# Second layer's front: context products of 129 columns per half, summed over the tiles in PSUM

## The chip, the core and the metric

The kernel runs on one core of a Trainium2 chip. Its time is the device time of one execution in microseconds (us); three runs of the kernel before gave a median of 2431.36 us (2429.86 to 2431.77).

## The reference, cut to what matters

Two layers of a graph network work on 2500 nodes of 256 features. Each layer has a graph part, a linear attention over all nodes, and a mixture of experts. The change is in the second layer's linear attention, whose sum over all nodes is `context`:

```python
q = jnp.einsum('bnc,oc->bno', x, Wq).reshape(B, N, h, d).transpose(0, 2, 1, 3)
kv = jnp.einsum('bnc,oc->bno', x, Wkv).reshape(B, N, 2, h, d)
k = kv[:, :, 0].transpose(0, 2, 1, 3)
v = kv[:, :, 1].transpose(0, 2, 1, 3)
q = jax.nn.elu(q) + 1.0
k = jax.nn.elu(k) + 1.0
k_sum = k.sum(axis=2)
D_inv = 1.0 / jnp.maximum(jnp.einsum('bhnd,bhd->bhn', q, k_sum), 1e-06)
context = jnp.einsum('bhnd,bhne->bhde', k, v)
attn = jnp.einsum('bhnd,bhde->bhne', q, context) * D_inv[..., None]
```

There are h = 8 heads of d = 32 features. Only k and v of the same head meet: of the 256 x 256 sum of k times v, the kernel needs the eight 32 x 32 blocks on the diagonal, and beside them the sum of k itself (`k_sum`).

## The kernel before

The program is a row of stages, each a function with a block of its own, and all engines meet at a barrier between two stages. The change is in `front1`, which runs from about 1260 to 1405 us. The nodes are cut into T = 20 tiles of 128. For each tile TensorE turns the normalised rows (`turn`, into `p_t`), multiplies them by the weights of k and v (`p_kv`, 512 columns, line 1799), of q (`p_q`, line 1805), of the graph part's scores (16 further columns of `p_q`, line 1809) and of the graph part's features (`p_h`, 512 columns, line 1818). All is fp32, and each fp32 product stands as two records in the trace, with two weight loads.

VectorE and ScalarE make the features of k and q: `take(t)` on VectorE writes `neg`, the negative part, and `v_m`, which is v with rows past the last node zeroed and a 257th column of ones (`live`); ScalarE takes the exponential of `neg` (line 1759); `features(t)` on VectorE writes `k_f` (line 1668) and `qT`. `context_product(t)` then multiplies each 128-feature half of `k_f` by all 257 columns of `v_m` (line 1789) into `p_c`, and VectorE adds the 2 x 257 columns of `p_c` to `context` in SBUF (line 1677, `add_context`).

The order on each engine is the order of the code. In round t TensorE issues `p_kv`, `p_q`, the scores, `turn(t + 1)`, `context_product(t - 1)` and `p_h`. VectorE issues `take(t)`, `norm(t + 2)`, `features(t)` and `add_context(t - 1)`. The waits that matter: `kv_used`, set by the `k_f` instruction, lets TensorE overwrite `p_kv` in the next round and lets the context product start; `c_ready` tells VectorE that `p_c` is full, and `c_used` tells TensorE that it has been added.

Ahead of the loop VectorE clears `context` (line 1685) and makes `w_a`, the weights of the scores, on which TensorE's first round waits (`wa_ready`). Behind it VectorE copies the diagonal blocks from `context` to `cb` (lines 1712 and 1713) and finds the range of the scores; ScalarE and SyncE store `z`, and the barrier ends the stage. TensorE's last product of the stage (`spread`, line 1824) goes to `p_c` too.

Of the kernel before, what the change touches and what calls it, by code (L numbers as in the profile page):

```python
# [8 lines left out]
ALU = mybir.AluOpType  # L9
# [4 lines left out]
P = 128  # L14
N = 2500
T = -(-N // P)
NP = T * P
LAST = N - (T - 1) * P
D = 256
# [8 lines left out]
H = 8  # L28
DH = D // H
# [1505 lines left out]
def front1(nc, io, st):  # L1535

    with ExitStack() as ctx:
        sb, ps, sem = tensors(nc, ctx)
# [12 lines left out]
        live = sb("live1", [P, T])  # L1551
        row = sb("row1", [P, 2, ROW1])
        neg = sb("neg1", [P, 2, 2 * D])
        k_f = sb("k_f1", [P, 2, D])
        v_m = sb("v_m1", [P, 2, D + 1])
        context = sb("context1", [P, 2, D + 1])
        ends = sb("ends1", [P, 2 * H])
        end = sb("end1", [2 * H, 1])
        diag = sb("diag1", [2 * H, 2 * H])
        ones = sb("ones1", [2 * H, P])  # L1560
# [7 lines left out]
        p_kv = ps("p_kv1", [P, 512])  # L1568
        p_q = ps("p_q1", [P, 512])
        p_c = ps("p_c1", [P, 2, 512])  # L1570
# [15 lines left out]
        neg_ready = sem("neg_ready1")  # L1586
        exp_ready = sem("exp_ready1")
        c_ready = sem("c_ready1")
        c_used = sem("c_used1")
        row_stored = [sem(f"row_stored{u}") for u in range(2)]  # L1590
        ends_ready = sem("ends_ready1")
        ends_turned = sem("ends_turned1")
# [1 line left out]
        spread = sem("spread1")  # L1594
# [36 lines left out]
        def _(dve):  # L1631
            link = Link(dve, dv)
# [17 lines left out]
            def take(t):  # L1650
                u = t % 2
                dve.wait_ge(kv_ready, t + 1)
                if t:
                    dve.wait_ge(exp_ready, t)
                dve.tensor_scalar(neg[:, u, 0:D], p_kv[:, 0:D], 0.0, None, ALU.min)
                link.inc(dve.tensor_scalar(v_m[:, u, 0:D], p_kv[:, D:], live[:, t:t + 1], None, ALU.mult))
                link.inc(dve.tensor_copy(v_m[:, u, D:D + 1], live[:, t:t + 1]))
                dve.wait_ge(q_ready, t + 1)
                dve.tensor_scalar(neg[:, u, D:], p_q[:, 0:D], 0.0, None, ALU.min).then_inc(neg_ready, 1)
                if t >= 2:  # L1660
                    dve.wait_ge(row_stored[u], 16 * (t // 2))
                dve.tensor_copy(row[:, u, HF:], p_q[:, D:D + H])
                dve.tensor_copy(st.s_all[:, t * 2 * H:(t + 1) * 2 * H], p_q[:, D:D + 2 * H]).then_inc(s_taken, 1)
# [6 lines left out]
                dve.scalar_tensor_tensor(out=st.qT[:, t * D:(t + 1) * D], in0=p_q[:, 0:D], scalar=0.0, in1=neg[:, u, D:],  # L1670
                                         op0=ALU.max, op1=ALU.add).then_inc(q_used, 1)

            def add_context(t):
                dve.wait_ge(c_ready, t + 1)
                if t:
                    dve.wait_ge(c_used, t)
                dve.tensor_tensor(context[:, :, :], context[:, :, :], p_c[:, :, 0:D + 1], ALU.add).then_inc(c_used, 1)

            norm(0)
            norm(1)  # L1680
            link(dve.tensor_tensor(diag_p[:, :], st.ident[:, :], st.iota[:, :], ALU.mult))
            link(dve.tensor_reduce(st.iota_p[:, :], diag_p[:, :], AX, ALU.add))
            link(dve.memset(live[:, :], 1.0))
            link(dve.tensor_copy(live[:, T - 1:T], st.rowmask[:, :]))
            link(dve.memset(context[:, :, :], 0.0))
            link(dve.memset(st.cb[:, :, :], 0.0))
            link(dve.memset(ones[:, :], 1.0))
            dve.wait_ge(w_in, 64)
# [8 lines left out]
            for t in range(T):  # L1697
                take(t)
                if t + 2 < T:
                    norm(t + 2)  # L1700
                features(t)
                if t:
                    add_context(t - 1)
            add_context(T - 1)
            dve.wait_ge(c_used, T)
            dve.wait_ge(s_taken, T)
            dve.wait_ge(dv, link.base + link.k)

            for g in range(4):
                r = slice(g * DH, (g + 1) * DH)  # L1710
                for c in range(2):
                    link.inc(dve.tensor_copy(st.cb[r, c, g * DH:(g + 1) * DH], context[r, c, (4 * c + g) * DH:(4 * c + g + 1) * DH]))
                    link.inc(dve.tensor_copy(st.cb[r, c, P + g:P + g + 1], context[r, c, D:D + 1]))

            s3 = st.s_all[:, :].rearrange("p (t c) -> p c t", t=T)[:, 0:H, :]
            link.inc(dve.tensor_reduce(ends[:, 0:H], s3, AX, ALU.max))
# [5 lines left out]
            link(dve.tensor_scalar(diag[:, :], st.ident[0:2 * H, 0:2 * H], end[:, 0:1], None, ALU.mult))  # L1722
            dve.sem_inc(diag_ready, 1)
            dve.wait_ge(spread, 1)
            link(dve.tensor_copy(ends[:, :], p_c[:, 0, 0:2 * H]))
            link.inc(dve.tensor_copy(st.s_max[:, :], ends[:, 0:H]))
            link(dve.tensor_tensor(span[:, :], ends[:, 0:H], ends[:, H:], ALU.add))
            link(dve.tensor_scalar(st.s_unit[:, :], span[:, :], 1.0 / S_RANGE, 1.0, ALU.mult, ALU.max))
# [39 lines left out]
        def _(pe):  # L1768
            for c in range(3):
                n = min(P, NSLOT - c * P)  # L1770
                last = pe.transpose(p_c[0:n, 0, c * P:(c + 1) * P], st.dloc[:, c * P:c * P + n], st.ident[:, :])
# [11 lines left out]

            def context_product(t):
                pe.wait_ge(kv_used, t + 1)
                if t:
                    pe.wait_ge(c_used, t)
                for c in range(2):
                    last = pe.matmul(p_c[:, c, 0:D + 1], k_f[:, t % 2, c * P:(c + 1) * P], v_m[:, t % 2], start=True, stop=True)
                last.then_inc(c_ready, 1)  # L1790

            turn(0)
            for t in range(T):
# [4 lines left out]
                for k in range(K):  # L1798
                    last = pe.matmul(p_kv[:, :], halves[k], w_kv[:, k], start=k == 0, stop=k == K - 1)
# [8 lines left out]
                for k in range(K):  # L1808
                    last = pe.matmul(p_q[:, D:D + 2 * H], halves[k], w_a[:, k], start=k == 0, stop=k == K - 1)
# [7 lines left out]
                for k in range(K):  # L1817
                    last = pe.matmul(p_h[:, :], halves[k], w_h[:, k], start=k == 0, stop=k == K - 1)
# [2 lines left out]
            pe.wait_ge(ends_ready, 1)  # L1821
            pe.transpose(p_q[0:2 * H, 0:P], ends[:, :], st.ident[:, :]).then_inc(ends_turned, 1)
            pe.wait_ge(diag_ready, 1)
            pe.matmul(p_c[:, 0, 0:2 * H], ones[:, :], diag[:, :], start=True, stop=True).then_inc(spread, 1)


def segment_bound(nc, io, st):
# [858 lines left out]
def program(nc, io):  # L2686
    with ExitStack() as ctx:
# [61 lines left out]
        with ExitStack() as gat:  # L2749
# [12 lines left out]
            st.b_p1 = gat.enter_context(nc.sbuf_tensor("b_p1", [P, D], F32))  # L2762
            st.w_in1 = gat.enter_context(nc.semaphore("w_in_o1"))
            front1(nc, io, st)
            segment_bound(nc, io, st)
            attend(nc, io, st)
# [44 lines left out]
```

## Time and profile before

| | |
|---|---|
| median of three runs | 2431.36 us |
| profiled execution, first to last instruction | 2432.3 us |
| TensorE busy over the span | 2103.5 us (86%) |
| VectorE busy over the span | 1491.2 us (61%) |
| `front1`: first products to the start of the next stage | 1260.0 to 1406.0 us |
| its loop: second tile's `p_kv` to the last `add_context` | 1282.4 to 1394.7 us |

The profile is one execution; its times count from its first instruction. PE is TensorE's products and PEld its weight loads, DVE is VectorE, ACT ScalarE, SPq SyncE's queue. The timeline merges neighbouring instructions of one kind into a row: its start, the time to the end of the last one, and how many there were. Ends of products are modelled, so the time of a product in a stream is read from start to start. "idle" in brackets is how long the engine did nothing before the row, and what ended it.

### The profile page before, as it was taken

The page shows a single profiled execution, that of the slowest core. Times are in us where ns is not written, and L with a number is a line of the kernel's source. Part 1 is how long each engine was busy: PE and PEld are TensorE (multiplying, and loading weights), DVE is VectorE, ACT ScalarE, POOL GpSimd, SP SyncE. Part 2 cuts the span into 40 slices and gives each one's busy share as a digit, 9 for nine tenths or more (in the row PEclk, how much of TensorE's full clock was granted, in tenths as well). Part 3 has the DMA queues.
Part 4 walks back from the last instruction along what each step waited for, and adds up shares of the span by engine and source line. Part 5 has one row for each costly group of instructions (what it writes and reads, how often), then busy time and mean ns, then how long its engine had stood idle before and what let it go on. Part 6 is the DMA issues. An engine that isn't in the chain of part 4 may idle for free. (4 is left out here: it accounts for less than half of the span.)

```text
span 2432.3 us, 31951 instructions
## 1 busy us (share of the span) xinstructions
PE 2103.5 (86%) x9692; PEld 1341.8 (55%) x9692; DVE 1491.2 (61%) x2938; ACT 737.7 (30%) x1962; POOL 974.7 (40%) x976
## 2 busy tenths in 40 slices
PE   4869996888899898699959958888887889999999
PEld 2346663444444446566636536666666766565665
DVE  8997777777787865433345558888887761211211
ACT  2511111111111113033312245555554232323232
POOL 4900004777666650055540067777776320000000
PEclk9989998999999998599979979999999989999999
DMA  3012223333333353433341178888888300000000
GB/s 113 31 59 98 98 93 95 103 102 102 95 94 95 94 75 102 156 53 57 57 102 44 44 210 243 240 239 239 239 240 199 113 1 1 9 9 1 9 9 8
DMA packets 118886, 241.54 MB, mean 99 GB/s; under 512 B 23255, under 2 KB 73182, under 8 KB 116030
## 3 DMA queue, kind: packets, MB, share of 16 engines
q0 software_dynamic: 56640, 160.17, 25.3%
q1 hardware_dynamic: 62078, 79.33, 10.1%
q8 instruction: 81, 1.33, 0.2%
q14 instruction: 87, 0.71, 0.1%
HBM read 196.24 MB, written 43.19 MB: 98 GB/s over the span
## 5 line engine op out<-in xcount | busy, mean ns | idle before, releaser
L672 POOL DMA_INDIRECT rows<-h_table,row_rel x372 | 361.4, 971 | 409.3 <-POOLq L95 268.1
L2137 PE MATMUL p_ag<-rows_g,oh_g 128*128 128x260 f32 x1488 | 398.7, 408 | 77.7 <-issue 57.6
L1980 POOL DMA_INDIRECT rows_g<-g_table,row_src x372 | 352.8, 949 | 255.1 <-POOLq L95 142.1
L2137 PEld LDWEIGHTS p_ag<-rows_g,oh_g 128*128 128x128 f32 x1488 | 256.9, 192 | 107.7 <-issue 74.3
L2503 DVE SCALAR_TENSOR_TENSOR x<-p_yf,cw_f,x 128x256 f32<-128x256 f32 (+1 forms) x160 | 66.4, 477 | 278.6 <-PE p_yf L2663 278.6
L927 PE MATMUL p_agg<-rows,oh 128*128 128x256 f32 x744 | 194.9, 396 | 24.8 <-DVE x L723 24.8
L2030 DVE TENSOR_TENSOR rows_g<-rows_g,p_e 128x2048 f32<-128x2048 f32 x93 | 211.8, 2278 | 0.0
L927 PEld LDWEIGHTS p_agg<-rows,oh 128*128 128x128 f32 x744 | 131.5, 190 | 88.6 <-DVE x L723 41.9
L792 DVE TENSOR_TENSOR fT<-a_sb,p_sel 128x512 f32<-128x512 f32 x200 | 128.6, 684 | 74.5 <-ACT a_sb L888 43.0
L2663 PE MATMUL p_yf<-f,h_f 128*128 128x256 f32 (+1 forms) x640 | 145.7, 381 | 0.8 <-ACT h_f L2555 0.8
L2613 PE MATMUL p_1f<-qT,f 128*128 128x512 f32 (+1 forms) x320 | 143.2, 591 | 0.5 <-ACT qT L2531 0.5
L2634 PE MATMUL p_2f<-h_f,f 128*128 128x512 f32 (+1 forms) x320 | 142.4, 588 | 0.4 <-DVEq L2450 0.4
L554 PE MATMUL p_h<-w_rel,xT_f 128*128 128x512 f32 x320 | 142.5, 598 | 0.0
L2013 DVE TENSOR_TENSOR acc<-acc,p_ag 128x520 f32 x186 | 128.8, 693 | 3.0 <-PE p_ag L2137 2.1
L2663 PEld LDWEIGHTS p_yf<-f,h_f 128*128 128x128 f32 (+1 forms) x640 | 117.6, 188 | 23.2 <-issue 5.9
L2555 ACT ACTIVATE h_f<-p_2f,par_b,par_g 128x512 f32<-128x512 f32 (+1 forms) x80 | 61.4, 767 | 219.8 <-PE p_2f L2634 219.8
L2120 PEld LDWEIGHTS p_n<-node_g,ohT_g 128*128 128x128 bf16 x1116 | 81.6, 98 | 74.4 <-DVE ohT_g L2003 15.3
L2061 ACT ACTIVATE away_g<-iota,dloc 128x128 f32<-128x128 f32 x372 | 117.5, 387 | 0.0
L536 ACT COPY h_out<-p_h 128x512 f32<-128x512 f32 x80 | 46.9, 587 | 223.1 <-PE p_h L554 223.1
L1410 POOL DMA_INDIRECT x_acc<-yo_g,to_tok x47 | 74.5, 1584 | 97.1 <-DMA x_acc<-yo_g,to_tok 80.8
L560 PE MATMUL p_rec<-hi_hot,lo_rec 125*128 125x372 f16 x680 | 110.8, 320 | 0.0
L985 PE MATMUL p_y<-fT,kvs 128*64 128x512 f32 x400 | 108.3, 619 | 0.0
(434 smaller groups left out, 3535.8 us busy)
## 6 DMA issues: line engine op xcount, KB each, us to landing
h_table<-h_out SPq DMA_DIRECT2D x20, 1024.0 KB, 4.2
where_g<-d_table SPq DMA_DIRECT2D x93, 128.0 KB, 4.3
w<-in_L_ffn_W SPq DMA_DIRECT2D x16, 512.0 KB, 8.8
rows<-h_table,row_rel POOLq DMA_INDIRECT x372
rows_g<-g_table,row_src POOLq DMA_INDIRECT x372
g_table<-row SPq DMA_DIRECT2D x20, 260.0 KB
f<-in_L_ffn_W SPq DMA_DIRECT2D x16, 256.0 KB, 5.9
xT_table<-xT SPq DMA_DIRECT2D x20, 128.0 KB, 1.7
```

What stands on the lines that cost most here:

```text
L554: last = pe.matmul(p_h[:, q], xT[:, t % XR, k * P:(k + 1) * P], st.w_rel[:, k, q * 512:(q + 1) * 512], start=k == 0, stop=k == K - 1)
L672: pool.indirect_dma_start(rows[:, r, j], None, st.h_rows, bass.IndirectOffsetOnAxis(ap=st.row_rel[:, at:at + 1], axis=0)).then_inc(gathere ...
L792: dve.tensor_tensor(fT[:, n % 3, i], a_sb[:, q % 2, i], p_sel[:, i], ALU.mult).then_inc(f_ready, 1)
L927: last = pe.matmul(p_agg[:, k % 3, 0:D], oh[:, r, j], rows[:, r, j], start=j % SUP == 0, stop=j % SUP == SUP - 1)
L1980: pool.indirect_dma_start(rows[:, r, j], None, st.g_table, bass.IndirectOffsetOnAxis(ap=st.row_src[:, at:at + 1], axis=0)).then_inc(gather ...
L2013: dve.tensor_tensor(out, out, p_a[:, k % NS, :, 0:HALF], ALU.add).then_inc(agg_added, 1)
L2030: dve.tensor_tensor(feats, feats, ex.unsqueeze(3).broadcast_to([P, BATCH, H, HID1]), ALU.mult).then_inc(msg_ready, 1)
L2061: last = nc.scalar.activation(away[:, s % 2, j], st.iota[:, :], ACT.Abs, bias=st.dloc[:, at:at + 1], scale=-1.0)
L2137: last = pe.matmul(p_a[:, k % NS, h, 0:HALF], oh[:, r, j], rows[:, r, j, h * HALF:(h + 1) * HALF], start=j % SUP == 0, stop=j % SUP == SUP ...
L2613: last = pe.matmul(p_1[:, s, 0:cols(n)], st.f1[:, e, k, s * P:(s + 1) * P], st.xnT[:, k, at:at + cols(n)], start=k == 0, stop=k == K - 1)
L2634: last = pe.matmul(p_2[:, s, 0:cols(n)], st.f2[:, e, k, s * P:(s + 1) * P], h1[:, n % 2, k, 0:cols(n)], start=k == 0, stop=k == K - 1)
L2663: last = pe.matmul(p_y[0:r, m % 2, j], h2[:, n % 2, s, j * P:j * P + r], st.f3[:, n % NE, s], start=s == 0, stop=s == K - 1)
```

## The change

The second half of `k_f` needs only the second half of v, and the first half only the first. `v_m` now holds each half of v with a column of ones of its own, 2 x 129 columns, and each half of `k_f` is multiplied by its own 129 columns. The products of all 20 tiles add up in `p_c` itself (`start` at the first tile alone, `stop` at the last), so `add_context`, its semaphore `c_used` and the clearing of `context` go; one copy takes `p_c` to `context` behind the loop. VectorE, which used to learn from `c_ready` in `add_context` that `v_m` had been read, now waits for `c_ready` in `take`. `spread` goes to `p_kv`.

```diff
@@ -1554,4 +1554,4 @@
         k_f = sb("k_f1", [P, 2, D])
-        v_m = sb("v_m1", [P, 2, D + 1])
-        context = sb("context1", [P, 2, D + 1])
+        v_m = sb("v_m1", [P, 2, 2, P + 1])
+        context = sb("context1", [P, 2, P + 1])
         ends = sb("ends1", [P, 2 * H])
@@ -1588,3 +1588,2 @@
         c_ready = sem("c_ready1")
-        c_used = sem("c_used1")
         row_stored = [sem(f"row_stored{u}") for u in range(2)]
@@ -1654,5 +1653,7 @@
                     dve.wait_ge(exp_ready, t)
+                if t >= 2:
+                    dve.wait_ge(c_ready, t - 1)
                 dve.tensor_scalar(neg[:, u, 0:D], p_kv[:, 0:D], 0.0, None, ALU.min)
-                link.inc(dve.tensor_scalar(v_m[:, u, 0:D], p_kv[:, D:], live[:, t:t + 1], None, ALU.mult))
-                link.inc(dve.tensor_copy(v_m[:, u, D:D + 1], live[:, t:t + 1]))
+                link.inc(dve.tensor_scalar(v_m[:, u, :, 0:P], p_kv[:, D:].rearrange("p (c e) -> p c e", c=2), live[:, t:t + 1], None, ALU.mult))
+                link.inc(dve.tensor_copy(v_m[:, u, :, P:P + 1], live[:, t:t + 1].unsqueeze(1).broadcast_to([P, 2, 1])))
                 dve.wait_ge(q_ready, t + 1)
@@ -1672,8 +1673,2 @@
 
-            def add_context(t):
-                dve.wait_ge(c_ready, t + 1)
-                if t:
-                    dve.wait_ge(c_used, t)
-                dve.tensor_tensor(context[:, :, :], context[:, :, :], p_c[:, :, 0:D + 1], ALU.add).then_inc(c_used, 1)
-
             norm(0)
@@ -1684,3 +1679,2 @@
             link(dve.tensor_copy(live[:, T - 1:T], st.rowmask[:, :]))
-            link(dve.memset(context[:, :, :], 0.0))
             link(dve.memset(st.cb[:, :, :], 0.0))
@@ -1701,6 +1695,4 @@
                 features(t)
-                if t:
-                    add_context(t - 1)
-            add_context(T - 1)
-            dve.wait_ge(c_used, T)
+            dve.wait_ge(c_ready, T)
+            link(dve.tensor_copy(context[:, :, :], p_c[:, :, 0:P + 1]))
             dve.wait_ge(s_taken, T)
@@ -1711,4 +1703,4 @@
                 for c in range(2):
-                    link.inc(dve.tensor_copy(st.cb[r, c, g * DH:(g + 1) * DH], context[r, c, (4 * c + g) * DH:(4 * c + g + 1) * DH]))
-                    link.inc(dve.tensor_copy(st.cb[r, c, P + g:P + g + 1], context[r, c, D:D + 1]))
+                    link.inc(dve.tensor_copy(st.cb[r, c, g * DH:(g + 1) * DH], context[r, c, g * DH:(g + 1) * DH]))
+                    link.inc(dve.tensor_copy(st.cb[r, c, P + g:P + g + 1], context[r, c, P:P + 1]))
 
@@ -1724,3 +1716,3 @@
             dve.wait_ge(spread, 1)
-            link(dve.tensor_copy(ends[:, :], p_c[:, 0, 0:2 * H]))
+            link(dve.tensor_copy(ends[:, :], p_kv[:, 0:2 * H]))
             link.inc(dve.tensor_copy(st.s_max[:, :], ends[:, 0:H]))
@@ -1785,6 +1777,4 @@
                 pe.wait_ge(kv_used, t + 1)
-                if t:
-                    pe.wait_ge(c_used, t)
                 for c in range(2):
-                    last = pe.matmul(p_c[:, c, 0:D + 1], k_f[:, t % 2, c * P:(c + 1) * P], v_m[:, t % 2], start=True, stop=True)
+                    last = pe.matmul(p_c[:, c, 0:P + 1], k_f[:, t % 2, c * P:(c + 1) * P], v_m[:, t % 2, c], start=t == 0, stop=t == T - 1)
                 last.then_inc(c_ready, 1)
@@ -1823,3 +1813,3 @@
             pe.wait_ge(diag_ready, 1)
-            pe.matmul(p_c[:, 0, 0:2 * H], ones[:, :], diag[:, :], start=True, stop=True).then_inc(spread, 1)
+            pe.matmul(p_kv[:, 0:2 * H], ones[:, :], diag[:, :], start=True, stop=True).then_inc(spread, 1)
```

The orders that follow are printed from the two programs; semaphores carry the name of the first stage that used them.

TensorE, from one round's `p_kv` to the next, before and then now (`xT_stored3` is `kv_used`, `made` is `c_used`):

```order
L1799 MATMUL p_kv<-w_kv,xT 128x512 [waits xT_stored3,xT_ready]
L1799 MATMUL p_kv<-w_kv,xT 128x512
L1805 MATMUL p_q<-xT,w_q 128x128 [waits qk_ready]
L1805 MATMUL p_q<-xT,w_q 128x128 x3
L1809 MATMUL p_q<-w_a,xT 128x16 x2
L1781 MATMUL p_t<-ident,xn 128x128 [waits xT_ready,xn_ready]
L1781 MATMUL p_t<-ident,xn 128x128
L1789 MATMUL p_c<-v_m,k_f 128x257 [waits made,xT_stored3]
L1789 MATMUL p_c<-v_m,k_f 128x257
L1818 MATMUL p_h<-w_h,xT 128x512 [waits xT_stored1]
L1818 MATMUL p_h<-w_h,xT 128x512
```

```order
L1789 MATMUL p_kv<-w_kv,xT 128x512 [waits xT_stored3,xT_ready]
L1789 MATMUL p_kv<-w_kv,xT 128x512
L1795 MATMUL p_q<-xT,w_q 128x128 [waits qk_ready]
L1795 MATMUL p_q<-xT,w_q 128x128 x3
L1799 MATMUL p_q<-w_a,xT 128x16 x2
L1773 MATMUL p_t<-ident,xn 128x128 [waits xT_ready,xn_ready]
L1773 MATMUL p_t<-ident,xn 128x128
L1779 MATMUL p_c<-v_m,k_f 128x129 [waits xT_stored3]
L1779 MATMUL p_c<-v_m,k_f 128x129
L1808 MATMUL p_h<-w_h,xT 128x512 [waits xT_stored1]
L1808 MATMUL p_h<-w_h,xT 128x512
```

Nothing moves; the two products of line 1789 (now 1779) have 129 columns instead of 257 and one wait less.

VectorE, one round in the middle of the loop, before and then now (`loop_added` is `exp_ready`, `xT_stored2` is `kv_ready`, `edges_in` is `c_ready`, `made` above is `c_used`; `v1_made` and, below, `made` in the row of line 1663 is the store of `row`):

```order
L1655 TENSOR_SCALAR neg<-p_kv 128x256 [waits loop_added,xT_stored2]
L1656 TENSOR_SCALAR v_m<-p_kv,live 128x256
L1657 COPY v_m<-live 128x1
L1659 TENSOR_SCALAR neg<-p_q 128x256 [waits lv_ready]
L1662 COPY row<-p_q 128x8 [waits v1_made]
L1663 COPY s_all<-p_q 128x16
L1647 TENSOR_SCALAR xn<-x,mean,rstd 128x256 [waits transposed]
L1668 SCALAR_TENSOR_TENSOR k_f<-p_kv,neg 128x256 [waits loop_added]
L1670 SCALAR_TENSOR_TENSOR qT<-p_q,neg 128x256
L1677 TENSOR_TENSOR context<-context,p_c 128x514 [waits made,edges_in]
```

```order
L1656 TENSOR_SCALAR neg<-p_kv 128x256 [waits edges_in,loop_added,xT_stored2]
L1657 TENSOR_SCALAR v_m<-p_kv,live 128x2x128
L1658 COPY v_m<-live 128x2
L1660 TENSOR_SCALAR neg<-p_q 128x256 [waits lv_ready]
L1663 COPY row<-p_q 128x8 [waits made]
L1664 COPY s_all<-p_q 128x16
L1646 TENSOR_SCALAR xn<-x,mean,rstd 128x256 [waits transposed]
L1669 SCALAR_TENSOR_TENSOR k_f<-p_kv,neg 128x256 [waits loop_added]
L1671 SCALAR_TENSOR_TENSOR qT<-p_q,neg 128x256
```

The addition at the round's end is gone, the first instruction has a third wait, and `v_m` is written in two pieces of 128 with two single columns.

VectorE behind the last round, before and then now:

```order
L1668 SCALAR_TENSOR_TENSOR k_f<-p_kv,neg 128x256 [waits loop_added]
L1670 SCALAR_TENSOR_TENSOR qT<-p_q,neg 128x256
L1677 TENSOR_TENSOR context<-context,p_c 128x514 [waits made,edges_in] x2
L1712 COPY cb<-context 32x32 [waits var_ready,lv_used,made]
L1713 COPY cb<-context 32x1
```

```order
L1669 SCALAR_TENSOR_TENSOR k_f<-p_kv,neg 128x256 [waits loop_added]
L1671 SCALAR_TENSOR_TENSOR qT<-p_q,neg 128x256
L1697 COPY context<-p_c 128x258 [waits edges_in]
L1704 COPY cb<-context 32x32 [waits var_ready,lv_used]
L1705 COPY cb<-context 32x1
```

Two additions of 514 columns, of which the second waits for the last product, give way to one copy of 258 columns with that wait.

## Rows read from the trace of the kernel before

**Rows 1.** The page, busy time of each engine over the whole span.

```profile
PE 2103.5 (86%) x9692; PEld 1341.8 (55%) x9692; DVE 1491.2 (61%) x2938; ACT 737.7 (30%) x1962; POOL 974.7 (40%) x976
```

**Rows 2.** Busy time by window, steady tiles; columns: length, busy per engine, clock, DMA.

```profile
1285.00:1390.00 105.00, 105.00 (x474) 68.64 (x474) 56.25 (x181) 26.79 (x54) 0.00 (x0) 1.00 0.12 46
```

**Rows 3.** Timeline of one steady tile; columns: start, duration, engine, line, operation, count, idle.

```profile
1324.84 1.05 PE L1805 MATMUL p_q<-xT,w_q 128*128 128x128 f32 x8
...
1325.38 0.48 DVE L1656 TENSOR_SCALAR v_m<-p_kv,live 128x256 f32<-128x256 f32 x1
...
1325.73 0.52 PE L1809 MATMUL p_q<-w_a,xT 128*128 128x16 f32 x4
...
1326.10 0.42 PE L1781 MATMUL p_t<-ident,xn 128*128 128x128 f32 x2
...
1326.28 0.42 DVE L1659 TENSOR_SCALAR neg<-p_q 128x256 f32<-128x256 f32 x1 [0.37 <-PE p_q L1809]
1326.35 1.03 PE L1789 MATMUL p_c<-v_m,k_f 128*128 128x257 f32 x4
...
1326.82 0.63 ACT L1759 ACTIVATE neg<-neg 128x512 f32<-128x512 f32 x1
...
1327.22 1.88 PE L1818 MATMUL p_h<-w_h,xT 128*128 128x512 f32 x4
1327.48 0.42 DVE L1668 SCALAR_TENSOR_TENSOR k_f<-p_kv,neg 128x256 f32<-128x256 f32 x1 [0.30 <-ACT neg L1759]
...
1328.51 0.19 PEld L1799 LDWEIGHTS p_kv<-w_kv,xT 128*128 128x128 f32 x1 [0.24 <-issue]
1328.93 1.88 PE L1799 MATMUL p_kv<-w_kv,xT 128*128 128x512 f32 x4
```

**Rows 4.** Groups of instructions by line, 1285 to 1394 us: VectorE, then weight loads.

```profile
L1677 DVE TENSOR_TENSOR context<-context,p_c 128x514 f32<-128x514 f32 x20 | 13.6, 682 | 1.3 <-PE p_c L1789 1.3
...
L1659 DVE TENSOR_SCALAR neg<-p_q 128x256 f32<-128x256 f32 x19 | 8.1, 425 | 7.0 <-PE p_q L1809 7.0
...
L1789 PEld LDWEIGHTS p_c<-v_m,k_f 128*128 128x128 f32 x80 | 13.6, 190 | 1.8 <-issue 0.8
```

**Rows 5.** Timeline, opening of the stage.

```profile
1271.50 0.49 DVE L1685 MEMSET context<- 128x514 f32 x1 [0.17 <-DVE live L1684]
...
1272.11 0.28 DVE L1686 MEMSET cb<- 128x264 f32 x1
...
1278.53 0.62 PE L1809 MATMUL p_q<-w_a,xT 128*128 128x16 f32 x4 [2.81 <-DVEq L1696]
```

**Rows 6.** Timeline, first tile to second, where TensorE waits for `k_f`.

```profile
1281.80 0.42 DVE L1668 SCALAR_TENSOR_TENSOR k_f<-p_kv,neg 128x256 f32<-128x256 f32 x1 [1.55 <-ACT neg L1759]
...
1282.34 0.30 PEld L1799 LDWEIGHTS p_kv<-w_kv,xT 128*128 128x128 f32 x2 [2.04 <-issue]
```

**Rows 7.** Timeline, end of the loop.

```profile
1392.83 1.10 PE L1789 MATMUL p_c<-v_m,k_f 128*128 128x257 f32 x4
...
1393.97 0.69 DVE L1677 TENSOR_TENSOR context<-context,p_c 128x514 f32<-128x514 f32 x1 [1.29 <-PE p_c L1789]
1394.69 0.17 DVE L1712 COPY cb<-context 32x32 f32<-32x32 f32 x1
```

**Rows 8.** Timeline, the first instruction of the next stage.

```profile
1405.99 0.19 DVE L1870 MEMSET zsum<- 128x160 f32 x1 [4.89 <-PEq L95]
```

**Rows 9.** Timeline and busy time by window, TensorE in the stage's opening.

```profile
1272.60 0.33 PEld L1799 LDWEIGHTS p_kv<-w_kv,xT 128*128 128x128 f32 x1 [0.52 <-issue]
...
1273.46 0.33 PEld L1799 LDWEIGHTS p_kv<-w_kv,xT 128*128 128x128 f32 x1 [0.52 <-issue]
...
1275.70:1278.50 2.80, 0.02 (x1) 0.00 (x0) 2.62 (x4) 0.00 (x0) 0.00 (x0) 1.00 0.00 0
```

**Rows 10.** Busy time by window, eight `p_2f` products twice, in the last stage.

```profile
1997.66:2003.02 5.36, 5.36 (x9) 2.34 (x10) 0.87 (x5) 1.01 (x2) 0.00 (x0) 0.68 0.00 0
2088.77:2092.20 3.43, 3.43 (x10) 1.51 (x9) 1.66 (x4) 0.78 (x1) 0.00 (x0) 1.00 0.24 81
```

## The prediction

> **What bounds the kernel now.** I read the page first: TensorE is busy for 86% of the span [rows 1], but that is a mean over stages, and the change touches one of them. So I went to the busy time by window for the stage's loop. From 1285 to 1390 us TensorE is busy for 105.00 of 105.00 us at full clock, VectorE for 56.25, ScalarE for 26.79 [rows 2]. The loop is TensorE's: a microsecond less on TensorE is a microsecond less in the loop until another engine's chain is late, and VectorE work taken out of it is worth nothing by itself. Then I read the timeline of one tile from start to start, since the modelled ends of products overlap [rows 3], the groups by line for what is regular [rows 4], and the two ends of the loop, where VectorE is the one waited for [rows 5 to 7]. The next stage opens at 1405.99 us with VectorE having stood idle for 4.89 us before a barrier [rows 8]; no work of it runs ahead, so what the stage saves reaches the end of the program.
>
> **Part 1: half the columns in the context product.** There are 20 tiles, each with four records of line 1789 (two products, two records each). In the tile shown they start at 1326.35 and `p_h` starts at 1327.22: 0.87 us, 0.2175 us a record of 257 columns [rows 3]. The nearest row for 129 columns is `p_q` in the same tile, eight records of 128 columns with a full weight load each: from 1324.84 to 1325.73, 0.89 us, 0.111 us a record [rows 3]. So a tile saves 4 x (0.2175 - 0.111) = 0.426 us. Bounds: the slowest step of 128 columns is the transposes', two records from 1326.10 to 1326.35, 0.125 us each, and leaves 4 x 0.0925 = 0.37 us; the smallest step in the stage is that of 16 columns, four from 1325.73 to 1326.10, 0.0925 us, and would leave 0.50 us [rows 3]. I take 0.426, the row with the same shape of load and stream. Nineteen of these products stand inside rounds and the twentieth behind the last `p_h`, where VectorE waits for it [rows 7]; all twenty lie on TensorE's path. 20 x 0.426 = 8.5 us (7.4 to 10.0). Adding to PSUM in place of overwriting it is no new operation: two of the four records of every `p_h` do it, and the four take 1.71 us, 1327.22 to 1328.93, 0.43 us each for 512 columns, twice the 0.2175 us of 257 [rows 3], so I cost it at nothing.
>
> Does the path stay TensorE's? With the round shorter, `p_kv` of the next tile starts 0.43 us earlier: at 1328.50 instead of 1328.93, its first load at 1328.08 instead of 1328.51 [rows 3]. It needs `k_f` of this tile, whose start follows from `p_q` by way of `neg` (1326.28), the exponential (1326.82) and `k_f` (1327.48, 0.42 us long) and so ends at 1327.90 [rows 3]; none of that hangs on the context product. How fast TensorE answers is seen at the first tile, where it does wait: `k_f` ends at 1282.22 and the load starts at 1282.34, 0.12 us later [rows 6]. So the load could start at 1328.02, 0.06 us ahead of need, and the product, which can follow its load at once, has some 0.45 us in hand. The saving holds, and what is late next is this `k_f`.
>
> **Part 2: VectorE in the round.** `add_context`, 0.682 us x 20 [rows 4], ran after `qT`, while VectorE waited for `p_kv` anyway. Inside the loop its removal is worth 0. What is added: `v_m` in two pieces, `live` in two columns, a third wait ahead of the first instruction. Before `neg` of `p_q` VectorE stands idle 7.0 us in 19 tiles, 0.37 us each [rows 4]. That covers them. From below nothing is saved; from above `v_m` could take twice its 0.48 us [rows 3], which would push `neg` by 0.48 - 0.37 = 0.11 us and with it `k_f`, still inside the 0.45 us. I take 0. The wait for `c_ready` in `take(t)` is for the context product of tile t - 2, issued in round t - 1, over 4 us before `p_kv` of round t is there [rows 3]; behind it the whole of `take` would queue, but it is never the last one. SyncE's stores of `row` are issued as before, each round 0.43 us sooner.
>
> **Part 3: the opening.** Clearing `context` starts at 1271.50 and the next memset at 1272.11: 0.61 us [rows 5]. It lies in VectorE's chain to `w_a`, for which TensorE waits until 1278.53 [rows 5], and everything in the first tile follows from there. Worth 0.61 us, all of it on the path (bounds 0.49, its own duration, and 0.61).
>
> **Part 4: the end.** The last addition takes 0.69 us, and the copies to `cb` start behind it [rows 7]. In its place a copy of 258 columns out of PSUM: nearest row `k_f`, 256 columns out of PSUM in 0.42 us [rows 3]. Gain 0.69 - 0.42 = 0.27 us, between 0 (as long as the addition) and 0.5 (as long as a copy of 32 columns, 0.17 us [rows 7]). I take 0.26. `spread` in another bank costs the same.
>
> **The sum.** 8.5 + 0.6 + 0.3 = 9.4 us. The profiled execution spans 2432.3 us, 0.9 us more than the median of the runs, so the time of a run lies at the span or just under it. 2432.3 - 9.4 = 2422.9 for an execution like the profiled one, 2431.4 - 9.4 = 2422.0 for the median of runs. I predict 2422.0 us. By the bounds of the parts the gain is 7.9 to 11.1 us, 2420.3 to 2423.5.
>
> One cost has no term. The last stage loses time where the clock is at its lower level when products start: eight `p_2f` products took 5.36 us at a mean clock of 0.68, and eight others 3.43 us at full clock [rows 10], a difference of 1.9 us. Where such dips fall may change as the program behind the stage comes 9.4 us sooner. I add 2 us to either side: the likeliest case's own range is 2418.5 to 2425.5.
>
> **Rivals.** *The weight load sets the step.* A load of line 1789 is recorded at 0.190 us [rows 4]; if products of 129 columns can't hide it, the step is 0.190 and not 0.111, the loop gives 80 x 0.0275 = 2.2 us, the sum is 2.2 + 0.6 + 0.3 = 3.1 and the time 2428.3 us: within 0.2%. Against it: `p_q` loads 128 x 128 weights for each record too, recorded just as long, and steps by 0.111 us [rows 3]. For it: `p_q` loads constant weights, `k_f` is fresh; I see no way in which that matters. The Trainium skill ("TensorE: Matmul & The Clock Gate", Measured speedup vs the span model) has a stricter rule: a weight load overlaps products in flight only where their row groups differ. These are full-array products; by that rule the load (128/1.2 = 107 ns by the section on LDWEIGHTS, an estimate) would stand in series with the product. The 257-column record steps by 0.2175 us and the 128-column one by 0.111 us [rows 3], which leaves no room for it, so the trace disagrees. Chance 5%.
>
> *`k_f` becomes the bound.* The load's margin is 0.06 us. If starting the load late delays the product by as much, or the three waits and the split writes of `v_m` cost VectorE much more than the idle 0.37 us, TensorE waits for `k_f` in every tile. For half of the 0.43 us to be lost, the chain must grow by 0.45 + 0.21 = 0.66 us from `neg` to `k_f`. Then the loop gives 4.3 us, the sum is 5.2 and the time 2426.2. Chance 6%.
>
> *Slower, by the clock.* This takes one mechanism: TensorE, now waiting for `k_f` each tile, gets the lower clock. A load of the 512-column products steps by 0.86 us in the opening (1272.60 to 1273.46, at half clock) [rows 9] and by 0.43 us in the loop [rows 3], so a round of 5.4 us takes 10.8. The gain of 9.4 us is gone when 1.7 rounds run at the lower level; with four of them the time is 2422.0 + 21.6 = 2443.6. For it: only that TensorE loses its unbroken stream. Against it: in the opening TensorE stood idle for 2.8 us (1275.7 to 1278.5) and the granted clock stayed at 1.00 [rows 9], far more than any gap of a tile here. Chance 2%.
>
> **How the numbers follow.** The forecast has 87%, the load 5%, `k_f` 6%, the clock 2%. A measurement of this kernel can tell 0.2%, 4.9 us, from no change. Faster by more than that means under 2426.5: the forecast nearly whole, and half or more of the `k_f` case, 0.90. Within 0.2%: the load case and the rest, 0.07. Slower: 0.03. The range is 2418.5 to 2427.0: the likeliest case's own, taken up to the `k_f` case; it leaves out the load case, the clock and some of the tail.
>
> **What would show it.** In the profile after: a round of 5.38 us instead of 5.81, TensorE without an idle gap in the loop, records of the context product stepping by 0.11 us; VectorE's wait for `p_kv` in a round about 0.25 us longer (the addition gone, the round shorter); the wait for `p_q` still there; TensorE's wait for `w_a` ending 0.6 us sooner; the copy of `p_c` at 0.4 us; the next stage's first instruction at 1396.6 us in place of 1405.99. I am wrong if TensorE shows waits for `k_f` beyond the first tile, if the step is over 0.125 us, if the clock in the loop is below 1.00, or if the stage is 9 us shorter and the program is not.

## The result, and the profile after

The changed kernel takes 2422.91 us (median of five runs, 2418.66 to 2425.19) against 2431.77 us for the kernel before (2429.86 to 2432.94). The ratio is 0.9959, 95% interval 0.9947 to 0.9972: faster by 8.9 us. The forecast was 2422.0 us, a gain of 9.4.

The profiled execution spans 2423.5 us. First the loop, by window; columns as in [rows 2].

```profile
1290.00:1380.00 90.00, 90.00 (x440) 58.44 (x439) 42.21 (x150) 24.91 (x51) 0.00 (x0) 1.00 0.14 51
```

TensorE is still busy for all of it at full clock, so nothing else has become late. VectorE, relieved of the additions, is down from 54% to 47% of the time. One tile of the timeline, to be read against [rows 3]:

```profile
1323.54 1.05 PE L1795 MATMUL p_q<-xT,w_q 128*128 128x128 f32 x8
...
1324.99 0.42 DVE L1660 TENSOR_SCALAR neg<-p_q 128x256 f32<-128x256 f32 x1 [0.35 <-PE p_q L1799]
1325.05 0.61 PE L1779 MATMUL p_c<-v_m,k_f 128*128 128x129 f32 x4
...
1325.50 1.88 PE L1808 MATMUL p_h<-w_h,xT 128*128 128x512 f32 x4
...
1326.18 0.42 DVE L1669 SCALAR_TENSOR_TENSOR k_f<-p_kv,neg 128x256 f32<-128x256 f32 x1 [0.30 <-ACT neg L1751]
...
1326.79 0.19 PEld L1789 LDWEIGHTS p_kv<-w_kv,xT 128*128 128x128 f32 x1 [0.24 <-issue]
1327.22 1.88 PE L1789 MATMUL p_kv<-w_kv,xT 128*128 128x512 f32 x4
```

From `p_c` at 1325.05 to `p_h` at 1325.50 the four records take 0.45 us, where they took 0.87. From `p_kv` at 1321.83 to `p_kv` at 1327.22 a round takes 5.39 us (5.81 before). `k_f` ends at 1326.60 and the next load starts at 1326.79, on time. VectorE's groups over the loop, to be read against [rows 4]:

```profile
L1657 DVE TENSOR_SCALAR v_m<-p_kv,live 128x256 f32<-128x256 f32 x20 | 9.5, 476 | 0.0
L1656 DVE TENSOR_SCALAR neg<-p_kv 128x256 f32<-128x256 f32 x20 | 8.5, 425 | 41.4 <-PE p_kv L1789 41.3
...
L1660 DVE TENSOR_SCALAR neg<-p_q 128x256 f32<-128x256 f32 x20 | 8.5, 424 | 6.7 <-PE p_q L1799 6.7
...
L1658 DVE COPY v_m<-live 128x2 f32<-128x2 f32 x20 | 3.2, 158 | 0.0
```

`v_m` in two pieces costs the 476 ns it cost in one, its two columns of ones 158 ns (144 before). The wait for `p_q`, in which these hide, is still 0.35 us a tile. The wait for `p_kv`, where the additions were, rose from 2.02 us a tile (36.3 in 18 rounds) to 2.17 (41.3 in 19). The row before:

```profile
L1655 DVE TENSOR_SCALAR neg<-p_kv 128x256 f32<-128x256 f32 x18 | 7.6, 425 | 36.3 <-PE p_kv L1799 36.3
```

The opening and the end, to be read against [rows 5 to 8]:

```profile
1273.48 0.15 DVE L1679 COPY live<-rowmask 128x1 f32<-128x1 f32 x1
1273.75 0.28 DVE L1680 MEMSET cb<- 128x264 f32 x1
...
1280.17 0.62 PE L1799 MATMUL p_q<-w_a,xT 128*128 128x16 f32 x4 [0.86 <-DVEq L1690]
...
1283.98 0.30 PEld L1789 LDWEIGHTS p_kv<-w_kv,xT 128*128 128x128 f32 x2 [2.04 <-issue]
```

```profile
1385.41 0.42 DVE L1669 SCALAR_TENSOR_TENSOR k_f<-p_kv,neg 128x256 f32<-128x256 f32 x1 [0.54 <-ACT neg L1751]
...
1385.92 0.19 PEld L1779 LDWEIGHTS p_c<-v_m,k_f 128*128 128x128 f32 x1 [0.24 <-DVE k_f L1669]
1386.35 0.61 PE L1779 MATMUL p_c<-v_m,k_f 128*128 128x129 f32 x4
...
1386.99 0.43 DVE L1697 COPY context<-p_c 128x258 f32<-128x258 f32 x1 [0.83 <-PE p_c L1779]
1387.55 0.17 DVE L1704 COPY cb<-context 32x32 f32<-32x32 f32 x1
...
1398.54 0.19 DVE L1860 MEMSET zsum<- 128x160 f32 x1 [4.90 <-PEq L95]
```

Where the time went, section by section, from the starts of the same instructions in both timelines:

| section | before, us | after, us | gain | forecast |
|---|---|---|---|---|
| ahead of the stage (to the clearing of `acc`) | 1260.01 | 1262.31 | -2.30 | 0 |
| to `rstd` | 9.42 | 9.42 | 0 | 0 |
| `rstd` to the `w_a` product | 9.10 | 8.44 | 0.66 | 0.61 |
| to the second tile's `p_kv` | 3.84 | 3.84 | 0 | 0 |
| to the last context product | 110.46 | 102.34 | 8.12 | 8.1 |
| to the first copy to `cb` | 1.86 | 1.20 | 0.66 | 0.69 |
| to the next stage's first instruction | 11.30 | 10.99 | 0.31 | 0 |
| **stage** | 145.98 | 136.23 | 9.75 | 9.4 |
| behind it | 1026.3 | 1025.0 | 1.3 | 0, plus or minus 2 |
| span | 2432.3 | 2423.5 | 8.8 | 9.4 |

The stage gave what was forecast, part by part. The 0.31 us of the tail came from the clock, which was at its lower level for the two short products there (`ends`, `spread`) before and at its higher one after; the change did not earn it, since `after_again` takes 11.31 us there. The windows of those products, before and then after:

```profile
1397.30:1399.20 1.90, 0.99 (x3) 0.59 (x3) 0.60 (x3) 0.00 (x0) 0.00 (x0) 0.50 0.00 0
```

```profile
1390.20:1391.70 1.50, 0.67 (x3) 0.38 (x3) 0.55 (x3) 0.00 (x0) 0.00 (x0) 1.00 0.00 0
```

What was not forecast is the size of the scatter outside the stage: 2.3 us more ahead of it, in code that the change doesn't touch.

### The profile page after: what moved, and what is told of

It is laid out like the page before. It is cut to its first block and busy times, and to the rows that moved or that the text cites. A ratio compares the mean times of both kernels' runs of the same rounds, so it can differ in the third digit from the quotient of the medians.

```text
span 2423.5 us, 31893 instructions
## 1 busy us (share of the span) xinstructions
PE 2097.4 (87%) x9692; PEld 1336.6 (55%) x9692; DVE 1479.4 (61%) x2918; ACT 737.4 (30%) x1962; POOL 974.6 (40%) x976
```

## The experiments

Three times are read in each profile: where the stage starts (the clearing of `acc`), its length, and what is behind it; the loop runs from the second tile's `p_kv` to the last context product. `before_again`, `late2`, `late3` and `cols65` ran once each, so only their stages are compared, not their whole times.

| kernel | starts at | stage | loop | behind |
|---|---|---|---|---|
| before | 1260.01 | 145.98 | 110.46 | 1026.3 |
| before_again | 1258.61 | 145.97 | 110.45 | 1026.1 |
| cols_only | 1258.96 | 136.88 | 102.63 | 1028.5 |
| psum_only | 1257.26 | 145.20 | 110.32 | 1022.7 |
| after | 1262.31 | 136.23 | 102.34 | 1025.0 |
| after_again | 1256.68 | 136.81 | 102.31 | 1025.5 |
| late2 | 1263.47 | 136.54 | 102.33 | 1026.7 |
| late3 | 1260.08 | 138.05 | 103.77 | 1024.6 |
| cols65 | 1260.78 | 136.75 | 102.31 | 1022.1 |
| open_short | 1262.10 | 133.73 | 102.34 | 1022.4 |
| before_twice | 1343.08 | 145.90 | 110.60 | 1120.6 |
| psum_twice | 1337.56 | 145.22 | 110.31 | 1122.6 |

**Which half of the change is the gain?** `cols_only` is the kernel before with the narrow products alone; the additions and the clearing of `context` stay, over 258 columns now instead of 514:

```diff
-        v_m = sb("v_m1", [P, 2, D + 1])
+        v_m = sb("v_m1", [P, 2, 2, P + 1])
...
-                dve.tensor_tensor(context[:, :, :], context[:, :, :], p_c[:, :, 0:D + 1], ALU.add).then_inc(c_used, 1)
+                dve.tensor_tensor(context[:, :, :], context[:, :, :], p_c[:, :, 0:P + 1], ALU.add).then_inc(c_used, 1)
...
-                    last = pe.matmul(p_c[:, c, 0:D + 1], k_f[:, t % 2, c * P:(c + 1) * P], v_m[:, t % 2], start=True, stop=True)
+                    last = pe.matmul(p_c[:, c, 0:P + 1], k_f[:, t % 2, c * P:(c + 1) * P], v_m[:, t % 2, c], start=True, stop=True)
```

> Kernel before with 129-column context products only; VectorE still adds 2 x 129 columns to context after every tile, context is still cleared, every product overwrites p_c. Theory A (TensorE's columns are the gain, the additions were hidden): the loop from the second tile's p_kv to the last context product shortens by 8.1 us as in the changed kernel (110.46 to 102.3), the end by a further 0.5 to 0.8 (shorter product, shorter addition), the opening not at all; stage 145.98 to about 137.1 us, ratio to before about 0.996. Rival B (taking the additions and their waits off VectorE is the gain): the loop stays above 108 us and the ratio is 0.999 to 1.

Ratio 0.996 (0.9946 to 0.9974), 2426.24 us against 2435.12. The loop is 102.63 us with all twenty additions still in it, the stage 136.88, and every round between is 5.39 us long as in the changed kernel. The 0.29 us over 102.34 are at the last product. The opening, from which nothing was expected, gave 0.27 us, because the clearing is shorter; the tail gave the clock's 0.32 us, as above. The end of its loop:

```profile
1381.67 1.88 PE L1818 MATMUL p_h<-w_h,xT 128*128 128x512 f32 x4
...
1383.12 0.41 DVE L1677 TENSOR_TENSOR context<-context,p_c 128x258 f32<-128x258 f32 x1
...
1383.65 0.52 PEld L1789 LDWEIGHTS p_c<-v_m,k_f 128*128 128x128 f32 x4 [0.93 <-DVE k_f L1668]
1383.68 0.68 PE L1789 MATMUL p_c<-v_m,k_f 128*128 128x129 f32 x4
```

`p_h` lets TensorE go at 1383.39 (1.72 us after its start), but the load of the last product starts at 1383.65, 0.12 us behind the end of the addition before it (1383.53): the row names `k_f`, the later wait is the one for `c_used`.

`psum_only` is the other half, the changed kernel with wide products:

```diff
-                    last = pe.matmul(p_c[:, c, 0:P + 1], k_f[:, t % 2, c * P:(c + 1) * P], v_m[:, t % 2, c], start=t == 0, stop=t == T - 1)
+                    last = pe.matmul(p_c[:, c, 0:D + 1], k_f[:, t % 2, c * P:(c + 1) * P], v_m[:, t % 2], start=t == 0, stop=t == T - 1)
```

> Changed kernel with 257-column products on all of v_m, summed in PSUM over the tiles, one copy of 514 columns at the end, no additions, no clearing of context. Theory A: the loop stays at 110.5 us, the opening gives 0.66, the end 0; stage 145.3 us, ratio about 0.9997, not to be told from 1. Rival B: the loop falls by most of 8 us with the additions gone, ratio 0.996.

Its loop is 110.32 us and its stage 145.20 us, 0.78 shorter than before, as theory A has it; B falls. The loop's 0.14 us are the same wait for `c_used`, which the kernel before has too and this one hasn't. The sum over tiles in PSUM is worth what it takes out of the two ends, where VectorE is waited for, and nothing in a round. But the whole runs came out at a ratio of 0.9985 (0.9975 to 0.9994), 3.7 us and not 0.8, and that interval leaves out the 0.9997 expected. Two more runs below go after this disagreement.

**Is the scatter outside the stage the change's?**

> The changed kernel once more. Theory A: stage 136.2 us give or take 0.5 by where the clock's lower level falls in the opening and end; what lies before the stage (1262.3 us) and behind it (1025.0 us) varies by some 2 us from execution to execution in both kernels, so the ratio is 0.996. Rival C: the change itself made the part before the stage 2.25 us longer; then it starts at 1262 us or later again.

> The kernel before once more, for a second profile: where its stage starts and how long it is. Theory A: stage 146.0 us within 0.5, its start anywhere from 1258 to 1263 us. Rival C (the 2.25 us ahead of the stage belong to the change): its start again within 0.5 us of 1260.0.

The changed kernel again: ratio 0.9955 (0.9943 to 0.9967), 2423.46 us, the stage now at 1256.68 and 136.81 us long. The 2.3 us ahead of the stage were not the change's: over the ten profiles of the table that share a time of about 2430 us the start lies between 1256.7 and 1263.5, whatever the kernel. The stage's own 0.6 us between two executions of one kernel are the clock's: in the second one `p_h` of the first tile ran at the lower level (0.28 us) and so did the tail (0.32). Ahead of that `p_h` TensorE had stood idle for 1.73 us; its four records take 3.35 us instead of 1.88:

```profile
1274.55 0.63 PE L1799 MATMUL p_q<-w_a,xT 128*128 128x16 f32 x4 [1.73 <-DVEq L1690]
...
1275.48 3.35 PE L1808 MATMUL p_h<-w_h,xT 128*128 128x512 f32 x4
```

> The kernel before against itself. If the differences between whole runs beyond the stage's are scatter of the rest of the program, the ratio's interval holds 1, its median may still lie some us off, and the stage is 146.0 us again. If a run's place in the rounds or its build biases the comparison, the ratio lies beside 1.

> 257 columns summed in PSUM once more: it came out 3.7 us faster than the kernel before in whole runs, while its stage is 0.8 us shorter. Theory A (scatter of the rest of the program): the ratio comes nearer 0.9997, stage 145.2 us again. Rival I (the change makes the rest of the program about 3 us faster, by where buffers or instructions lie): ratio 0.9985 again.

These two ran on another chip of the same kind, with a surprise: the kernel before took 2609.66 us there. (The runs from `late2` to `open_short` were on a third one, where it took 2435.09, as on the first.) Its stage was 145.90 us long, within 0.1 us of before. That close a match is partly luck: the loop and the section ahead of it were 0.24 us longer there, all of it in the first rounds, and the tail 0.34 shorter. The steady rounds take 5.81 us on both. Busy times by window, first the kernel before on the first chip, then on this one (two stages of indirect gathers: 390 to 930 us, and 1420 to 1860):

```profile
200.00:390.00 190.00, 187.81 (x777) 120.25 (x775) 137.32 (x327) 35.56 (x61) 0.00 (x0) 1.00 0.26 97
...
1420.00:1860.00 440.00, 375.20 (x2416) 295.51 (x2417) 375.51 (x608) 248.94 (x885) 333.07 (x352) 0.98 0.84 241
```

```profile
200.00:390.00 190.00, 187.68 (x776) 120.14 (x774) 137.33 (x327) 35.55 (x61) 0.00 (x0) 1.00 0.26 97
...
1420.00:1860.00 440.00, 320.31 (x1842) 231.59 (x1840) 283.04 (x536) 177.51 (x617) 227.79 (x241) 0.91 0.59 174
```

Ahead of the first gather the two agree within 0.2 us of busy time. In the gathers the rate falls: 174 GB/s instead of 241 in the window above. The first gather stage takes 594 us from first to last product instead of 511, the second 559 instead of 473, together 169 of the 177 us. Whether the chip or the hour makes the difference is not shown; TensorE's stage is untouched by it. Against itself the kernel before gave 0.9998 (0.9975 to 1.002). `psum_twice` gave 0.9985 again, with an interval of 0.9966 to 1.0004 and a stage of 145.22 us. Rival I is not refuted: 0.8 us of the 3.7 are shown, and the rest may be scatter or a small gain elsewhere. Whole runs against the stage's own gain leave the question open: `after_again` gained 11.7 us where its stage gained 9.2, `open_short` 14.1 where its stage gained 12.2, but `cols_only` 8.9 where its stage gained 9.1, and the first comparison 8.9 where the stage gained 9.75. One source of scatter can be named. From the last `p_mo` product of the stage behind the gathers to the first product `p_yf<-f,h_f` of the last stage the kernel before took 40.2 us in one profile and 37.2 in another, `cols_only` 40.3, `late2` 38.2, and `psum_only`, after and after_again 37.0; the clock rises there at different moments:

```profile
1989.50:1994.50 5.00, 5.00 (x6) 2.05 (x7) 0.76 (x5) 0.78 (x1) 0.00 (x0) 0.51 0.00 0
1994.50:1999.50 5.00, 4.57 (x22) 2.98 (x21) 1.13 (x6) 2.29 (x3) 0.00 (x0) 0.83 0.00 0
1999.50:2004.50 5.00, 5.00 (x11) 2.13 (x10) 0.00 (x0) 1.55 (x2) 0.00 (x0) 0.83 0.00 0
```

```profile
1983.90:1988.90 5.00, 5.00 (x15) 2.26 (x13) 0.46 (x3) 1.19 (x2) 0.00 (x0) 0.78 0.00 0
1988.90:1993.90 5.00, 4.57 (x19) 2.76 (x20) 1.12 (x6) 2.65 (x4) 0.00 (x0) 1.00 0.00 2
1993.90:1998.90 5.00, 4.20 (x13) 1.68 (x11) 0.00 (x0) 2.75 (x4) 0.00 (x0) 1.00 0.00 0
```

Both start 20 us behind that product. TensorE is starting again after an idle stretch (7.79 us in before, up to 1986.62); the mean granted clock of the windows is 0.51, 0.83 and 0.83 in before and 0.78, 1.00 and 1.00 in after. Whether the changed timing favours the early rise or it was luck, these runs don't settle.

**How much does `k_f` have in hand?** `late2` and `late3` hold VectorE up in each tile between `v_m` and `neg` of `p_q`, by two and three copies of:

```diff
+                dve.tensor_scalar(idle[:, 0], p_kv[:, 0:D], 0.0, None, ALU.min)
```

> Changed kernel with two more VectorE instructions a tile between v_m and neg of p_q (minimum of 256 columns of p_kv into a buffer that nothing reads). They start 0.34 us apart, VectorE is idle 0.35 us there, so neg of p_q, the exponential and k_f come 0.33 us later. Theory A (only the p_kv product's start counts, 0.45 us in hand): the loop stays at 102.3 us. Rival D (the 0.07 us ahead of the p_kv load is the margin): each of 18 rounds loses 0.26 us, the loop is 107.0 us.

> The same with three more VectorE instructions a tile: k_f comes 0.67 us later. Theory A: 0.22 us lost in each of 18 rounds, loop 106.3 us. Rival D: 0.60 us lost, loop 113.1 us, longer than the 110.46 us of the kernel before. Either way TensorE waits for k_f by name in every round; Rival E (the gap brings the lower clock): granted clock in the loop under 1.00.

`late2` lost nothing: loop 102.33 us. Two tiles, first of `late2`, then of `late3`:

```profile
1331.74 0.42 DVE L1663 TENSOR_SCALAR neg<-p_q 128x256 f32<-128x256 f32 x1
...
1332.86 0.42 DVE L1672 SCALAR_TENSOR_TENSOR k_f<-p_kv,neg 128x256 f32<-128x256 f32 x1 [0.22 <-ACT neg L1754]
...
1333.40 0.19 PEld L1792 LDWEIGHTS p_kv<-w_kv,xT 128*128 128x128 f32 x1 [0.31 <-issue]
1333.76 1.88 PE L1792 MATMUL p_kv<-w_kv,xT 128*128 128x512 f32 x4
```

```profile
1329.54 0.41 DVE L1664 TENSOR_SCALAR neg<-p_q 128x256 f32<-128x256 f32 x1
...
1329.99 0.63 ACT L1755 ACTIVATE neg<-neg 128x512 f32<-128x512 f32 x1 [0.36 <-DVE neg L1664]
...
1330.65 0.43 DVE L1673 SCALAR_TENSOR_TENSOR k_f<-p_kv,neg 128x256 f32<-128x256 f32 x1 [0.22 <-ACT neg L1755]
...
1331.19 0.30 PEld L1793 LDWEIGHTS p_kv<-w_kv,xT 128*128 128x128 f32 x2 [0.64 <-issue]
1331.22 1.96 PE L1793 MATMUL p_kv<-w_kv,xT 128*128 128x512 f32 x4
```

In `late2` the load came late (idle 0.31 instead of 0.24 us before it, 0.36 us ahead of its product instead of 0.43) and the product on time, so rival D falls: the load's start is no margin. The test was milder than meant, since two instructions moved `neg` by 0.22 us and `k_f` by 0.13, not by 0.33; the load came 0.07 us late, which rival D would have charged to every round (some 1.3 us of the loop). In `late3` TensorE does wait, product 0.03 us behind load. The loop is 103.77 us, 0.08 us a tile more, not the 0.22 expected: counted from the end of `p_kv`, three instructions moved `neg` by 0.55 us, not 0.67, and `k_f` by 0.46, since ScalarE absorbed 0.09 (it had been held up by its own copy of `xT`). 0.46 - 0.08 leaves `k_f` a margin of about 0.38 us where the prediction put 0.45. The loss sits in the first record of `p_kv`: it starts 0.03 us behind its load, but the second record starts 0.51 us later instead of 0.43. The prediction had let the product follow its load at no cost. The wait was not shown as a wait for `k_f` by name, but as idle time of the load. The granted clock stayed at 1.00, so rival E falls for waits as short as these.

```profile
1290.00:1380.00 90.00, 90.00 (x432) 56.19 (x432) 57.00 (x201) 26.39 (x50) 0.00 (x0) 1.00 0.13 48
```

**Would fewer columns give more?** `cols65` takes 65 columns a half in all tiles but the first; most of v's sum is left out.

```diff
-                    last = pe.matmul(p_c[:, c, 0:P + 1], ..., v_m[:, t % 2, c], ...)
+                    n = P + 1 if t == 0 else 65
+                    last = pe.matmul(p_c[:, c, 0:n], ..., v_m[:, t % 2, c, 0:n], ...)
```

> Changed kernel in which the context product of every tile but the first has 65 columns a half in place of 129 (most of v's sum is left out). Theory A (the step of 129 columns, 0.112 us, is the stream's; below it the load sets a floor of about 0.0925 us, the step of the 16-column products): a tile saves 4 x 0.019 = 0.08 us, the loop is 100.9 us. Rival F (no floor from the load, the stream alone): step 0.056, loop 98.2 us. Rival G (the load already sets the step of 129 columns): loop 102.3 us, nothing saved.

Theory A was wrong here and G right: loop 102.31 us, nothing saved. Loads and products of one tile:

```profile
1334.45 0.53 PEld L1780 LDWEIGHTS p_c<-v_m,k_f 128*128 128x128 f32 x4
...
1334.56 0.56 PE L1780 MATMUL p_c<-v_m,k_f 128*128 128x65 f32 x4
...
1334.89 0.30 PEld L1809 LDWEIGHTS p_h<-w_h,xT 128*128 128x128 f32 x2
...
1334.95 1.94 PE L1809 MATMUL p_h<-w_h,xT 128*128 128x512 f32 x4
...
1336.72 0.59 PE L1790 MATMUL p_kv<-w_kv,xT 128*128 128x512 f32 x1
```

The products start 0.39 us apart from `p_c` to `p_h`, 0.06 less than with 129 columns, but the loads from 1334.45 to 1334.89 still take 0.11 us each, and `p_h` pays the 0.06 back (1.77 us to the next `p_kv` instead of 1.72). A full 128-column load every 0.11 us is the pace of this row of short products; 129 columns of fp32 lie just at it.

Read record by record, the same step stands in rows of still fewer columns. The four products of `w_a`, 16 columns each, step by 0.03, 0.11, 0.11 and 0.11 us, and from the second on each starts 0.03 us behind its own load. Sixteen products of 8 columns in the last stage (`p_2f<-w_g_f,qT`, 1988.28 to 1989.87 in after) step by 0.03 once and then by 0.11 every time. So theory A's floor of 0.0925 us was a mean that hid 0.11, and the trace of the kernel before had it already. All these loads have 128 columns, so no run separates the load from a fixed cost of each load and its product; against such a cost speak products with 33-column loads in the first layer (`p_y<-kx,v`, four of them from 671.30 to 671.47 in after, 0.04 us each), but they start in pairs 0.01 us apart, so they are no clean test. Nor is every single load 0.11 us behind the one before: the first load of `turn` starts 0.03 us behind the last of `w_a`, the second 0.14 behind the first. The Trainium skill ("TensorE: Matmul & The Clock Gate", LDWEIGHTS) puts a load at its column count over 1.2 GHz, an estimate of 107 ns for 128 columns, and this trace agrees with it over the row (17 loads in 1.85 us), though not load by load.

**A shorter opening.** The changed kernel's opening is VectorE's chain to `w_a` and then ScalarE's table of the exponential, 1.28 us ahead of `k_f`. `open_short` takes both out:

```diff
+            link(dve.memset(live[:, :], 1.0))
+            link(dve.tensor_copy(live[:, T - 1:T], st.rowmask[:, :]))
             dve.wait_ge(sd_ready, 1)
...
                 features(t)
+                if t == 2:
+                    link(dve.tensor_tensor(diag_p[:, :], st.ident[:, :], st.iota[:, :], ALU.mult))
+                    link(dve.tensor_reduce(st.iota_p[:, :], diag_p[:, :], AX, ALU.add))
+                if t == 3:
+                    link(dve.memset(st.cb[:, :, :], 0.0))
+                    link(dve.memset(ones[:, :], 1.0))
...
             take_x(0)
+            nc.scalar.activation(table[:, :], st.rowmask[:, 0:1].broadcast_to([P, T]), ACT.Exp)
```

The six instructions named are gone from their old place.

> Changed kernel with a shorter opening: live is made while VectorE waits for ScalarE's root, diag_p, iota_p, cb's and ones' clearing go into rounds 2 and 3 where VectorE waits 2.2 us for p_kv, and ScalarE loads the table of the exponential by one idle exponential between the first two copies of xT. By the rows of the changed kernel: w_a is ready up to 1.6 us sooner, of which TensorE can use 0.9 to 1.7 us (its own products before end then), and the second tile's p_kv no longer waits for k_f, 1.2 us. Stage 136.2 to 133.5 us, 134.5 at worst, loop unchanged at 102.3. Rival H: the table is loaded again at the first real exponential, and only the 0.9 to 1.6 us come.

The stage is 133.73 us, 2.5 shorter than after's: 1.49 us between `rstd` and the `w_a` product net of the 0.13 that `live` costs ahead of it, 1.32 to the second tile's `p_kv`, less 0.31 us lost again to the clock in the tail. Rival H falls: the table is loaded once, at 1273.61, and not again at the first real exponential (1279.76). Ratio 0.9937 (0.9923 to 0.995), 2420.96 us against 2435.09: the fastest kernel of the study, though its interval overlaps the changed kernel's.

## Why the prediction was right

- *The loop is TensorE's.* Right. `cols_only` and `psum_only` show it: 7.8 us of the loop for the columns alone, 0.14 for the additions alone, and none of that inside a round. Together they give 8.12: with narrow products the wait for the addition costs 0.29 us, with wide ones 0.14. That the last product waits for the addition before it (0.14 us in the kernel before) I had not seen.
- *0.426 us a tile from the step of 0.111.* Right: a round fell from 5.81 to 5.39 us, 0.42, and 19 x 0.42 + 0.14 = 8.12 is the loop's gain; the last product gave 0.5. The number came from `p_q`, a row with the same load and nearly the same columns, so it held whichever of the two sets the step. The reason was not known: the bound of 0.50 us a tile took 0.0925 us as a possible step, and `cols65` shows that with 128-column loads the step does not fall under 0.11. That bound was out of reach; 129 columns lie at the knee.
- *The rival of the weight load.* It was nearer the cause than its 5% says: the loads set a pace, as far as `cols65` and the rows of 16 and 8 columns show it, but of 0.11 us and not of the 0.190 that the trace records for one. The rule on row groups that is set beside it stands on its page of the Trainium skill under "The mechanism", not under the section named; the steps after the change (0.11 us with a full load each) disagree with it as those before did.
- *`k_f` is in time, with 0.45 us in hand.* Right in kind, the margin measured at about 0.38: a product that starts right behind its load loses 0.08 us in its first record. The 0.06 us of the load was no bound, as said.
- *VectorE's edits in the round cost nothing.* Right; the idle 0.37 us fell to 0.35. VectorE's wait for `p_kv` grew by about 0.15 us a tile and not by 0.25: the addition had started before `qT` ended, so it had kept VectorE for 0.60 us more and not for 0.68.
- *Opening 0.61.* Measured 0.66: the clearing took the gap behind it along.
- *End 0.26 plus the last product.* The copy took the 0.43 us expected, but 0.13 us pass before the first copy to `cb` starts where 0.03 did (every profile that ends with the copy has this 0.13, also with 514 columns in `psum_only`, and every one that ends with the addition has 0.03, also with 258 in `cols_only`; so it isn't the width, and more no run shows). The product gave 0.50 us where 0.43 was counted and the copy 0.16 where 0.26 was. That the sum came out at 0.66 against 0.69 is in part luck.
- *The term without a price.* The margin of 2 us for the rest of the program was meant for one product stage's clock. It was too small as a description of single runs, which scatter by 6.5 us in the first five and by 15.7 in eleven others of the changed kernel; the median stayed within it. Two slips did no harm: the lower end of the range by its own sum is 2420.3 - 2 = 2418.3 us and not 2418.5, and a run's time lies not under its profiled span but 1.7 to 2.0 us over it (2425.19 against 2423.5, 2432.67 against 2430.7).
- *The slower rival.* `late3` made TensorE wait in every tile and the clock stayed up, but by 0.08 us a tile only. The argument from the opening was weaker than it looked: there TensorE stood idle for 2.8 us before with the clock at 1.00 behind it, while in `after_again` an idle stretch of 1.73 us was followed by the lower level. What longer waits in the loop would do to the clock, no run shows.

## What to carry to other kernels

In a stage where TensorE is busy all the time, count columns and loads: cutting columns pays until the step reaches the pace of the weight loads (0.11 us for 128 columns of fp32 here), and that pace is read from single records, not from the mean of a short row. Taking work off an engine that waits pays only at the two ends of the loop. Read the margin of the next chain from the start of the product, less what it loses behind a late load (0.08 us here), not from the start of its early load. Judge a change of a few us by the length of its stage in the profile, which repeats to a few tenths, before the time of whole runs, which here does not; what the change does outside the stage, its length can't show.

## What was not expected of the hardware

The same program took 2432 us on one chip and 2610 on another, nearly all of the difference in stages of gathers (594 against 511 us and 559 against 473), none in the steady rounds of the TensorE stage (5.81 us on both). In a row of fp32 products with a fresh 128-column load each, 65 columns were no faster than 129 (loop 102.31 against 102.34 us).
